# A one-core transformer layer: the order of the prologue rewritten, and the first head's maxima spread over the value products

## What is computed

```python
x = x + conv(_ln_c(x), w_qkv, b_qkv, w_proj, b_proj, rel_pos_h, rel_pos_w)
t = t + moe(_ln_t(t), w_router, wi, wo)          # 8 experts, top 2, capacity 40 rows a group

# conv: 12 heads of 32
qkv = x @ w_qkv + b_qkv
attn = einsum('bnd,bmd->bnm', q * scale, k)
attn = attn + rel_h[..., :, None] + rel_w[..., None, :]   # products of q with rel_pos_h and rel_pos_w
out = (softmax(attn) @ v) @ w_proj + b_proj
```

## Time and profile before

| | us |
|---|---|
| three runs | 624.33, 621.49, 623.77 |
| median | 623.77 |
| profiled execution | 622.83 |
| its span | 621.0 |
| TensorE busy | 596.5 (96%) |
| VectorE busy | 397.8 (64%) |
| ScalarE busy | 301.6 (49%) |
| GpSimd busy | 196.4 (32%) |

### The profile page before, as it was taken

The page is one execution under the profiler, slowest core; times in us unless marked ns, Lnnn a source line. Parts: engine busy times, 40 slices in busy tenths (PEclk is TensorE's granted clock), DMA queues, the critical chain, the costliest instruction groups (busy, mean ns, idle before and its releaser), DMA issues.

```text
span 621.0 us, 11960 instructions
## 1 busy us (share of the span) xinstructions
PE 596.5 (96%) x4457; PEld 506.4 (82%) x4457; DVE 397.8 (64%) x664; ACT 301.6 (49%) x419; POOL 196.4 (32%) x116
## 2 busy tenths in 40 slices
PE   1998999999999999999999999999999999999996
PEld 1786876666666666667988999999999999999994
DVE  6656767676676667633888985457654665467535
ACT  3555424454555545455556435354445554365523
POOL 0400047889888888898200000000000000000000
PEclk9999999999999999999989999999999999999999
DMA  8046054333234444103142443443453434442302
GB/s 267 8 86 128 3 115 98 73 65 65 60 80 84 85 85 85 39 2 102 34 158 70 161 153 123 141 154 119 131 165 94 155 142 152 152 147 83 115 0 103
DMA packets 37411, 63.35 MB, mean 102 GB/s; under 512 B 3864, under 2 KB 32894, under 8 KB 37246
## 3 DMA queue, kind: packets, MB, share of 16 engines
q1 hardware_dynamic: 37374, 62.83, 36.2%
HBM read 44.16 MB, written 1.57 MB: 74 GB/s over the span
## 4 chain that ended last, share of the span: by engine, by line
PE 91%; DVE 5%; ACT 2%; DMA 1%; SPq 1%; issue 1%; DVEq 0%
PE ps L769 20%; PE ps L785 20%; PE ps L552 14%; PE ps L561 10%; PE ps L462 8%; PE ps L538 8%; DVE rhalf L1135 2%; PE ps L492 1%; PE ps L795 1%; PE ps L703 1%; DMA onehot<-c_onehot 1%; PE ps L585 1%; PE ps L740 1%; PE ps L715 1%; PE ps L447 1%; PE ps L802 1%
## 5 line engine op out<-in xcount | busy, mean ns | idle before, releaser
L1135 DVE TENSOR_REDUCE rhalf<-ps 128x1 f32<-128x512 f32 x192 | 131.4, 691 | 40.9 <-PE ps L538 39.8
L928 ACT ACTIVATE prob<-ps 128x1024 f32<-128x1024 f32 x96 | 98.0, 1027 | 97.4 <-PE ps L552 88.1
L396 POOL TENSOR_TENSOR acc<-acc,prob 128x1024 f32<-128x1024 f32 x58 | 139.5, 2406 | 5.9 <-POOL acc L392 0.8
L552 PE MATMUL ps<-qst,kst 128*128 128x512 f32 x384 | 111.1, 395 | 0.0
L422 POOL CAST dpc<-dpt 80x1024 fp32r (+1 forms) x4 | 4.2, 1042 | 278.6 <-PE ps L803 203.2
L769 PE MATMUL ps<-xeh,wih 128*128 128x320 f32 (+1 forms) x288 | 89.8, 312 | 1.0 <-ACT xeh L990 1.0
L785 PE MATMUL ps<-hh,woh 128*128 128x320 f32 x288 | 89.3, 310 | 0.0
L785 PE MATMUL ps<-hl,woh 128*128 128x320 f32 x288 | 89.0, 309 | 0.0
L769 PE MATMUL ps<-xel,wih 128*128 128x320 f32 (+1 forms) x288 | 89.0, 309 | 0.0
L769 PE MATMUL ps<-xeh,wil 128*128 128x320 f32 (+1 forms) x288 | 89.0, 309 | 0.0
L785 PE MATMUL ps<-hh,wol 128*128 128x320 f32 x288 | 89.0, 309 | 0.0
(11 more groups left out here) (159 smaller groups left out, 908.2 us busy)
## 6 DMA issues: line engine op xcount, KB each, us to landing
raw_i<-in_L_ffn_wi SPq DMA_DIRECT2D x32, 576.0 KB, 4.9
raw_o<-in_L_ffn_wo SPq DMA_DIRECT2D x32, 576.0 KB, 4.0
xs<-in_x SPq DMA_DIRECT2D x8, 384.0 KB, 4.8
qst<-qh SPq DMA_DIRECT2D x12, 256.0 KB, 3.2
qst<-relh SPq DMA_DIRECT2D x12, 256.0 KB, 3.9
qst<-relw SPq DMA_DIRECT2D x12, 256.0 KB, 4.5
kst<-kp SPq DMA_DIRECT2D x12, 256.0 KB, 5.1
qst<-ql SPq DMA_DIRECT2D x12, 128.0 KB, 3.2
```

Source lines behind the costliest of these rows:

```text
L396: nc.gpsimd.tensor_tensor(acc[:, :], acc[:, :], prob[:, t % SLOT, :], ALU.add).then_inc(sum_add, 1)
L552: last = mm(bank(2 * (t % 2) + half), kst[b][:, part, t * P:(t + 1) * P], qst[b][:, part, half * BANK:(half + 1) * BANK], start=part == 0, ...
L928: run(prob[:, t % SLOT, :], ps[:, 2 * (t % 2) * BANK:2 * (t % 2 + 1) * BANK], ACT.Exp).then_inc(exp_done, 1)
L1135: ve.tensor_reduce(rhalf[:, p // 2, p % 2:p % 2 + 1], bank(4 + p % 2), AX_X, ALU.max).then_inc(max_red, 1)
```

## The change

It rewrites the prologue at six places and leaves the rest of the program as it was.

- Transfers: `ident` gets its own semaphore and goes between the second and the third transfer of x. `onehot` gets its own too and goes behind the q and k weights. Those weights come in four pieces: the columns of the first q product and of the first k product, then the rest.
- TensorE starts with 22 filler products of `ones`. It turns the first half of `xn`, then the tables, then makes three more fillers, then turns the second half. The wait on `bd_ready` goes from ahead of `qk(0)` to ahead of `qk(3)`; the banks of the q and k products rotate by one.
- ScalarE copies the first half's `xnh` ahead of the second `norm`. VectorE takes all six `xnl` ahead of the copies into `bqk` and `bd`, and no longer takes the first weights' low part: GpSimd does.
- The `relw` transposes write to PSUM with a stride, so that both copies out of it read rows and write runs of 16 numbers.
- `first_max` makes one score product a step, 8 in all; the other 8 stand two behind each of the first four value tiles, and `turn_max` stands behind the fifth.
- VectorE's order follows in the same way.

```diff
         FIRST = [
-            (ident[:, :], ident_c), (flip[:, :], flip_c),
+            (flip[:, :], flip_c),
...
-            (b6[:, :], b_qkv[0:2 * D].rearrange("(m p) -> m p", p=P)), (onehot[2 * SIDE:4 * SIDE, :], onehot_c),
+            (b6[:, :], b_qkv[0:2 * D].rearrange("(m p) -> m p", p=P)),
...
-        QK_BANKS = [6, 7, 4, 5]
+        QK_BANKS = [7, 4, 5, 6]
+        WARM = 22
...
-            return (rel[1][:, part, c, :].rearrange("p (r w) -> p w r", w=SIDE)[:, half * w:(half + 1) * w, :],
-                    b.rearrange("p (w r) -> p w r", w=w))
+            return (rel[1][:, part, c, :].rearrange("p (r w) -> p r w", w=SIDE)[:, :, half * w:(half + 1) * w],
+                    b.rearrange("p (r w) -> p r w", w=w))
...
                 sp.dma_start(xs[:, n * XT:(n + 1) * XT, :], x_v[:, n * XT:(n + 1) * XT, :]).then_inc(x_in[n], 16)
+                if n == 1:
+                    sp.dma_start(ident[:, :], ident_c).then_inc(ident_in, 16)
...
-            for dst, cols, arrived in ((wqk, slice(0, 2 * D), wqk_in), (wv, slice(2 * D, 3 * D), wv_in)):
-                sp.dma_start(dst[:, :, :], w_qkv.rearrange("(c p) n -> p c n", p=P)[:, :, cols]).then_inc(arrived, 16)
+            w_v = w_qkv.rearrange("(c p) n -> p c n", p=P)
+            for cols, arrived in ((slice(0, P), wqk_in[0]), (slice(D, D + P), wqk_in[0]),
+                                  (slice(P, D), wqk_in[1]), (slice(D + P, 2 * D), wqk_in[1])):
+                sp.dma_start(wqk[:, :, cols], w_v[:, :, cols]).then_inc(arrived, 16)
+            sp.dma_start(onehot[2 * SIDE:4 * SIDE, :], onehot_c).then_inc(onehot_in, 16)
+            sp.dma_start(wv[:, :, :], w_v[:, :, 2 * D:3 * D]).then_inc(wv_in, 16)
...
-            pool.wait_ge(wqk_in, 16)
             for i in range(2 * DC + 1):
+                if i == 0:
+                    pool.wait_ge(wqk_in[0], 32)
+                if i == 2:
+                    pool.wait_ge(wqk_in[1], 32)
...
                 nc.gpsimd.tensor_copy(high, raw).then_inc(w_hi, 1)
+                if i == 0:
+                    pool.wait_ge(w_hi, 1)
+                    nc.gpsimd.tensor_tensor(low, raw, high.bitcast(F32), ALU.subtract).then_inc(w_lo, 1)
...
+            def keep_warm(n):
+
+                for _ in range(n):
+                    mm(bank(7, P), ones[:, :], ones[:, :], start=True, stop=True)
+
+            pe.wait_ge(ones_set, 1)
+            keep_warm(WARM)
+            def turn_tables():
+
+                pe.wait_ge(first_in, 16 * len(FIRST))
...
+                if half == 0:
+                    pe.wait_ge(ident_in, 16)
                 turn(xn, X_TURNS[DC * half:DC * (half + 1)])
-
-            pe.wait_ge(bd_ready, 2)
+                if half == 0:
+                    turn_tables()
+                    keep_warm(3)
...
+                if n == 3:
+                    pe.wait_ge(bd_ready, 2)
...
+                    to = bank(2 + n % 2)[:, t * P:(t + 1) * P]
+                    if REL[n][0] == 1:
+                        to = bank(2 + n % 2).rearrange("p (r w) -> p w r", w=SIDE // 2)[:, t * HPG:(t + 1) * HPG, :]
+                    last = nc.tensor.transpose(to, rst[:, n % 2, t * P:(t + 1) * P], ident[:, :])
...
-                for p in range(2 * (n - 4), 2 * (n - 3)):
-                    max_scores(0, 0, 0, p)
+                max_scores(0, 0, 0, n - 4)
...
                 value_tile(t)
-                if t == 1:
+                if t < HALF:
+                    for p in range(NT + 2 * t, NT + 2 * t + 2):
+                        max_scores(0, 0, 0, p)
+                if t == HALF:
                     turn_max(0)
```

More of the change, by code:

```diff
@@ L179, in metaformer_layer @@
         x_in = [sem(f"x_in{n}") for n in range(NT // XT)]
-        first_in, later_in, wpj_in = sem("first_in"), sem("later_in"), sem("wpj_in")
-        wqk_in, wv_in, w_hi, w_lo, wp_hi, wp_lo = (sem(n) for n in ("wqk_in", "wv_in", "w_hi", "w_lo", "wp_hi", "wp_lo"))
+        ident_in = sem("ident_in")
+        first_in, later_in, wpj_in, onehot_in = sem("first_in"), sem("later_in"), sem("wpj_in"), sem("onehot_in")
+        wqk_in = [sem("wqk_in0"), sem("wqk_in1")]
+        wv_in, w_hi, w_lo, wp_hi, wp_lo = (sem(n) for n in ("wv_in", "w_hi", "w_lo", "wp_hi", "wp_lo"))
         raw_i_in = [sem("raw_i_in0"), sem("raw_i_in1")]
@@ L358, in _ @@
             nc.gpsimd.memset(ones[:, :], 1.0).then_inc(ones_set, 1)
-            pool.wait_ge(wqk_in, 16)
             for i in range(2 * DC + 1):
+                if i == 0:
+                    pool.wait_ge(wqk_in[0], 32)
+                if i == 2:
+                    pool.wait_ge(wqk_in[1], 32)
                 if i == 2 * DC:
                     pool.wait_ge(wv_in, 16)
-                raw, high, _ = weights(i)
+                raw, high, low = weights(i)
                 nc.gpsimd.tensor_copy(high, raw).then_inc(w_hi, 1)
+                if i == 0:
+                    pool.wait_ge(w_hi, 1)
+                    nc.gpsimd.tensor_tensor(low, raw, high.bitcast(F32), ALU.subtract).then_inc(w_lo, 1)
             pool.wait_ge(w_hi, 2 * DC + 1)
-            pool.wait_ge(first_in, 16 * len(FIRST))
+            pool.wait_ge(onehot_in, 16)
             nc.gpsimd.memset(qst[0][HD:2 * HD, 1, :].bitcast(F32), 0.0).then_inc(rows_set, 1)
@@ L433, in _ @@
             mm = nc.tensor.matmul
[L436 to L441, removed]
+            def keep_warm(n):
[5 more added lines that the diff above has]
+                pe.wait_ge(first_in, 16 * len(FIRST))
+                for kind in range(2):
+                    nc.tensor.transpose(bank(6)[:, NREL * kind:NREL * (kind + 1)],
+                                        rp[:, kind, :, :].rearrange("p a b -> p (a b)"), flip[:, :]).then_inc(rp_turned, 1)
+                nc.tensor.transpose(bank(6)[:, 2 * NREL:2 * NREL + 2 * DC], b6[:, :],
+                                    ident[0:2 * DC, 0:2 * DC]).then_inc(rp_turned, 1)
             def turn(src, banks):
@@ L860, in _, with turn_back @@
             run = nc.scalar.activation
-            def turn_back(dst, n, banks):
+            def turn_back(dst, n, banks, first=0):
                 for i, k in enumerate(banks):
-                    act.wait_ge(turned, 2 * DC * n + i + 1)
+                    act.wait_ge(turned, 2 * DC * n + first + i + 1)
                     run(dst[:, k % DC, (k // DC) * BANK:(k // DC + 1) * BANK], bank(k), ACT.Copy).then_inc(turn_act, 1)
@@ L877, in _ @@
             norm(xs, xn, 0)
+            turn_back(xnh, 0, X_TURNS[0:DC])
             norm(xs, xn, 1)
-            turn_back(xnh, 0, X_TURNS)
-            act.wait_ge(bd_ready, 2)
+            turn_back(xnh, 0, X_TURNS[DC:2 * DC], DC)
+            act.wait_ge(bd_ready, 1)
             def units(first, end):
@@ L1095, in _ @@
                 norm(xs, xn, LN_C_EPS, half, lambda t: dve.wait_ge(x_in[t // XT], 16))
+            dve.wait_ge(xn_dve, NT // 2)
+            dve.wait_ge(xn_act, NT // 2)
+            turn_back(xnl, xnh, 0, X_TURNS[0:DC])
+            turn_back(xnl, xnh, 0, X_TURNS[DC:2 * DC], DC)
             dve.wait_ge(bd_zero, 1)
@@ L1102, in _ @@
             last.then_inc(bd_ready, 1)
[L1103 to L1107, removed]
             def units(first, end):
@@ L1113, in units @@
                     if half == 0:
+                        if n == 0:
+                            dve.wait_ge(w_lo, 1)
                         weights_low(n // 2 + 1)
@@ L1169, in _ @@
             for n in range(4, 4 * DC):
-                reduce_max(0, 2 * (n - 4))
-                reduce_max(0, 2 * (n - 4) + 1)
+                reduce_max(0, n - 4)
                 rel_low(n)
-            whole_max(0)
             for t in range(NT):
@@ L1176, in _ @@
                 ve.tensor_tensor(vt[:, t, :], bank(V_BANKS[t % 4], D), bv[:, :], ALU.add).then_inc(v_dve, 1)
-                if t == 1:
+                if t < HALF:
+                    reduce_max(0, NT + 2 * t)
+                    reduce_max(0, NT + 2 * t + 1)
+                if t == HALF - 1:
+                    whole_max(0)
+                if t == HALF:
                     negate_max(0)
```

2 lines of the change are left out of this document (removed).

## The result

| | before | changed |
|---|---|---|
| median of 8 runs, us | 622.85 | 619.0 |
| lowest and highest | 620.38, 625.68 | 616.99, 619.16 |
| profiled execution | 622.83 | 619.1 |
| its span | 621.0 | 617.3 |

The ratio is 0.9932, with a 95% interval of 0.9914 to 0.9949: 4.2 us less, between 3.2 and 5.4 (the two medians alone lie 3.85 apart). Measured again (experiment e9) the changed kernel came out at 618.53 against 623.32, ratio 0.9917 (0.9896 to 0.9937), 5.2 us less by the ratio, between 3.9 and 6.5. Forecast were 618.3 and a gain of 5.05.

The account below looks back on a forecast made before the run. TensorE, busy 96% of the span, was taken as the bound, so gains come from its gaps, slow work or start waits. 2.3 + 4.4 - 1.65 = 5.05 us off gave 617.8 to 618.7, forecast 618.3, range 616.2 to 621.3.

Parts of the forecast that it names:

- Part 1: Start, to the first q product: from 18.15 to 15.85 us, a gain of 2.3 us, bounds 0.8 and 3.5.
- The share of `ident`: Start: `ident` ahead of x's last two transfers delays x's last pair by 0.25 us, bounds 0 and +0.5.
- The assumed rise in the fillers' pace: Start: the 22 fillers speed up after some 4.5 us and end near 8.3, ahead of the transposes; cost 0.
- Part 2: Position steps 4 to 11: steps of 1.87 instead of 2.06 us, a gain of 4.4 us, bounds 3.0 and 4.8.
- Part 3: Value tiles: the added score products lose 1.65 us before head 0, bounds 1.3 and 2.6.
- The 0.3 us for a late VectorE: Value tiles: VectorE enters behind, with the last `relw` and a reduction still to do; 0.3 us added.
- The maxima's way: Ahead of head 0: `mneg` leaves at about 76.7, its transfer having almost four microseconds until 80.55, so it is hidden.
- The router's clock: Router: the half-clock interval may fall elsewhere, 0.65 us less to 1.3 more; 0 taken, both put into the range.
- Rival 1: Steps and value tiles: the gap only moves, waits not being the two reductions'; gain 2.4, 620.9 us; chance 0.12.
- Rivals 2 and 3: Start: stays late, `first_in` or first weights late, 619.8 us (chance 0.12); or gains more, x early, 617.1 us (0.08).
- Rival 4: `relw` steps: strided PSUM writes slow 24 transposes; 0.21 us more each uses up the gain, 0.35 gives 627; chance 0.05.
- rival 5: Start: clock falls back in TensorE's two new pauses, transposes and first q product at half speed, at most 1.5 us.

Follow-up runs that it names:

- e9: The changed kernel itself, measured again: 618.53 us, ratio 0.9917.
- e1: The new start alone, everything behind the last q and k product as in the kernel before: 621.4 us, ratio 0.9968.
- e12: The changed kernel with the router's 48 products widened to 64 columns, measured again: 617.47 us, ratio 0.9904.
- e11: The kernel before with widened router products, `relw` in rows and the maxima spread, old start kept: 618.97 us, ratio 0.9932.
- e7: The changed kernel with GpSimd's difference for the first weights waiting until VectorE has written all its `xn`: 617.51 us, ratio 0.9916.
- e5: The changed kernel with the router's 48 narrow products widened to 64 columns: 617.05 us, ratio 0.9904.
- e6: The kernel before with the router's 48 narrow products widened to 64 columns: 622.03 us, ratio 0.9986.
- e3: The changed kernel with `relw` transposed in its old order and spread by the two copies, as before: 620.99 us, one time only.
- e2: The changed kernel with two score products a step again and none behind the value tiles, `relw` still in rows: 620.54 us, ratio 0.9939.
- e8: The changed kernel with both GpSimd's difference waiting for VectorE's `xn` and the router products widened to 64 columns: 616.11 us, ratio 0.9889.

## Why the prediction was right

**What bounds it.** Right. The chain's three places (the wait for `onehot`, VectorE in the steps, the value tiles) are the three at which the profile changed.

**Part 1, the start: 2.3 forecast, 2.07 in the two profiles, about 1.5 to 2.0 in times (e1, e12 against e11).** The order of events on the path came as worked out, each step within 0.3 us. Two terms were off, in opposite directions, and left the 0.2 us that were missing. The share of `ident` was sized at 0.25; the statistics ended at 11.00, where they had at 10.94, so it cost 0.06. And the meeting of GpSimd's difference with VectorE's `xn` was not in the sum: `xn` was complete at 14.01, by VectorE, where ScalarE's part ended at 13.61: 0.4 us, which e7 took back. The meeting came of a step off the path that was sized wrong: I had the first weights at 13 to 13.5 and their low part at 14.5 to 15.0, behind `xn`; GpSimd began with them at 11.64, and the low part was done at 13.23. The assumed rise in the fillers' pace had no row behind it, and their end (8.34, with 8.3 worked out) is luck to that extent: in the ten profiles with 44 of them they took anything from 6.52 to 7.98 us. The Trainium skill, "GPSIMD Engine Reference", section 8, names two kinds of VectorE instruction that contend with GpSimd: those with two inputs in SBUF, and those in a mode that uses both ports. I weighed only the first. The trace agrees for it: `mv`, which has two inputs in SBUF, took 0.71 us beside the difference in e5. `xn` has one input in SBUF, and was slowed 2.7 times; whether it runs in a mode of the second kind, no run here shows. The six GpSimd casts that the prediction leaned on tell little, as only the last one ran beside the three `xnl`.

That the times give less than the two profiles fits the profile of before, in which x and `onehot` came late. In e6, whose start is that of the kernel before, the tables were turned at 10.65 and the first q product started at 16.31, hardly later than e5's 16.27 with the new start:

```profile
10.65 0.47 PE L438 MATMUL ps<-flip,rp 63*128 63x63 f32 x2 [10.65 <-DMA onehot<-c_onehot]
```

e11, the third profile with the old start, has it at 17.59. So with one and the same start the first q product moves by up to 1.8 us with the transfers. A term read from one execution carries that, as the forecast's 2.3 does.

**Part 2, the steps: 4.4 forecast, 4.5 measured** (20.02 to 15.52). A step takes 1.82 to 1.91, forecast 1.87, with no wait on `rhalf`.

**Part 3, the value tiles: 1.65 of loss forecast, 1.5 measured** (13.61 to 15.08). The 0.3 us for a late VectorE did not come: its last `relw` is done at 65.35 and `vt` follows at once, for which e3 shows the need of the rows. The maxima's way is as said: `mneg`'s transfer leaves at 74.14, four microseconds ahead of head 0.

```profile
74.14 0.74 SPq L324 DMA_DIRECT2D qst<-mneg  x1
...
78.18 0.39 PE L568 MATMUL ps<-kst,qst 128*128 128x512 f32 x1
```

**The sum.** 5.05 forecast, 5.11 at the router's start, 5.0 between the widened kernels; 4.2 and 5.2 us in the two measurements as they are.

**The router's clock.** The term was named, with 0 taken and -0.65 to +1.3 in the range. In the profile it came to +1.46. What I sized wrong was the price: I let the half clock fall on the fillers alone, which are partly hidden, and it fell on the transposes and their fillers, which are not.

**The rivals.** Rival 1 fell (no wait on `rhalf` left). Rivals 2 and 3: `first_in` and the first weights were early enough; x came neither way. Rival 4 fell: the strided transposes cost 1 ns more on average, and hold TensorE for 0.41 us a step like the others. Of rival 5, the clock's fall in the new pauses is real, though only in some executions: e1, e2, e3 and e8 have it in their profiles, the changed kernel's own does not. From the first q product to step 4's products, where the clock stays up it takes 31.7 us, in e2 and e3 32.7 and 32.9, so it costs 1.0 to 1.2 us there. The rule that was weighed (the Trainium skill, "TensorE: Matmul & The Clock Gate", Part 4, transposes do not count as activity) would have made the first q products slow as a matter of course; in the changed kernel's profile the first four take 8.55 us, 8.56 before, all at the full rate.

## What to carry to other kernels

When two engines are level in a loop, moving work off the loop pays in full only if the next stretch does not inherit the backlog: cost a relief together with what is still queued at the boundary (here either cure alone gave 1.7 us and both 3.0). Add the gain up at the last place that the change touches and compare it with the end: a difference between the two places has its own cause, here a clock that falls in some executions. Before explaining part of a gain by the change, see whether executions of one kernel differ by as much.

## What the runs showed of the hardware

- In seven of the eight profiles in which the router's 48 matmuls are 8 columns wide (two groups of 24, one every 0.11 us without a gap), a stretch at half clock follows (granted 0.50, the level of 1.2 GHz); in the eighth, e7's, none does. In none of the six in which they are 64 columns wide does one follow, and they take 0.1 us more in all. By the medians that is worth 1.1 to 1.4 us here, in the kernel before as well.
- A transpose that writes PSUM with a stride of 64 bytes between its columns costs TensorE nothing measurable (287 against 286 ns, and 0.41 us for four in either form), and took 0.5 us each off ScalarE's and VectorE's copies of 512 columns.
- A GpSimd difference with two inputs in SBUF took 1.00 us (I had worked out 0.90), and stretched a VectorE `tensor_scalar` of 384 float32 from 0.47 to 1.26 us, or, in e5, a `scalar_tensor_tensor` of 4 float32 from 0.16 to 0.71 us and the `tensor_scalar` behind it to 0.72.
- With the new start, TensorE pauses for 1.4 to 2.0 us ahead of the second half's transposes. In the profiles of e1, e2, e3 and e8 a stretch at half clock follows, in those of the changed kernel, e5, e7, e9 and e12 none.
- All four transfers of x were issued by 3.3 us, and VectorE had its statistics of them done anywhere from 9.8 to 11.0 us in the fourteen profiles, in both orders of the start.
